# Keys written to memory by tile, contiguous marks as weights, and batches of 15 tiles (seven gathered) in 208 steps instead of 16 in 195

## The reference

```python
msg = relu(x[src] + edge_attr_32)                 # 400000 x 32
agg = segment_sum(msg, dst, num_segments=12500)   # 12500 x 32
h = (1.0 + eps[0]) * x + agg
x = layernorm(x + h @ W.T + b, axis=-1)
```

## Time and profile before

| what | value |
|---|---|
| median of three runs | 3029.05 us (3026.18 to 3032.44) |
| span of the profiled execution, first to last instruction | 2071.9 us |
| own time of the profiled execution | not recorded beside the span |
| TensorE busy | 2016.0 us, 46449 matmuls |
| VectorE, ScalarE, GpSimd busy | 1648.3, 1565.9 and 1519.9 us |
| TensorE's granted clock over the span | 0.993 of full speed |

### The profile page before, as it was taken

The page is one execution under the profiler, slowest core; times in us unless marked ns, Lnnn a source line. Parts: engine busy times, 40 slices in busy tenths (PEclk is TensorE's granted clock), DMA queues, the critical chain, the costliest instruction groups (busy, mean ns, idle before and its releaser), DMA issues. The chain is left out here.

```text
span 2071.9 us, 117127 instructions
## 1 busy us (share of the span) xinstructions
PE 2016.0 (97%) x46449; PEld 1922.5 (93%) x46449; DVE 1648.3 (80%) x4231; ACT 1565.9 (76%) x1616; POOL 1519.9 (73%) x1571
## 2 busy tenths in 40 slices
PE   4899999999999999999999999999999999999997
PEld 3899999999999999999999999999999999999994
DVE  7888778888888778888888877888888887788875
ACT  5777777777777777777777777777777777777773
POOL 6577777777777777777777777777777777777770
PEclk9999999999999999999999999999999999999998
DMA  6344454444444444544444444444444444444441
GB/s 163 84 111 113 113 114 114 112 110 109 110 111 112 112 113 114 114 110 110 110 110 110 114 112 113 112 114 109 110 110 110 111 113 113 111 114 114 110 110 34
DMA packets 236283, 228.68 MB, mean 110 GB/s; under 512 B 104218, under 2 KB 185556, under 8 KB 236062
## 3 DMA queue, kind: packets, MB, share of 16 engines
q1 hardware_dynamic: 186177, 202.59, 33.4%
q0 software_dynamic: 50080, 25.74, 13.3%
HBM read 225.43 MB, written 2.71 MB: 110 GB/s over the span
## 5 line engine op out<-in xcount | busy, mean ns | idle before, releaser
L541 POOL DMA_INDIRECT rows_all<-in_x,index x1565 | 1519.4, 971 | 502.8 <-issue 476.5
L1173 PE MATMUL found<-table,oh 128*128 128x128 bf16 x18720 | 1241.3, 225 | 11.5 <-issue 2.5
L1173 PEld LDWEIGHTS found<-table,oh 128*128 128x128 bf16 x18720 | 1168.1, 144 | 43.6 <-issue 20.0
L1012 ACT ACTIVATE oh<-keys,minus_lanes 128x1024 bf16<-128x1024 f16 x195 | 224.2, 1150 | 307.3 <-PE found L1173 294.5
L1154 PE MATMUL l<-xparts,oh 128*57 128x96 bf16 x18720 | 436.2, 207 | 0.9 <-ACT oh L1000 0.9
L1154 PEld LDWEIGHTS l<-xparts,oh 128*57 128x57 bf16 x18720 | 409.4, 108 | 14.0 <-issue 1.1
L993 ACT ACTIVATE oh<-slots,minus_lanes 128x1824 bf16<-128x1824 f16 x195 | 351.3, 1801 | 7.1 <-DMA slots<-slot_dram 7.1
L786 DVE COPY_PREDICATED rows_all<-mask,found 128x256 f32<-128x256 uint16 x780 | 343.1, 440 | 7.6 <-issue 1.4
L968 ACT CAST table<-l 128x768 bf16<-128x768 f32 x390 | 310.9, 798 | 39.7 <-PE l L1154 24.7
L1000 ACT ACTIVATE oh<-oh 128x1824 bf16<-128x1824 bf16 x195 | 335.7, 1721 | 0.0
L780 DVE TENSOR_TENSOR mask<-iota,side 128x32 f16<-128x32 f16 x195 | 37.5, 192 | 303.1 <-PE found L1173 291.0
(11 more groups left out here) (126 smaller groups left out, 906.5 us busy)
## 6 DMA issues: line engine op xcount, KB each, us to landing
slots<-slot_dram SPq DMA_DIRECT2D x195, 456.0 KB
msg<-in_edge SPq DMA_DIRECT2D x390, 128.0 KB
keys<-key_dram SPq DMA_DIRECT2D x195, 256.0 KB
rows_all<-in_x,index POOLq DMA_INDIRECT x1565
index<-in_src SPq DMA_DIRECT2D x195, 4.0 KB
key_dram<-key SPq DMA_DIRECT2D x195, 2.0 KB
slot_dram<-slot_row SPq DMA_DIRECT2D x195, 3.6 KB
oh<-in_x SPq DMA_DIRECT2D x3, 512.0 KB, 6.2
```

Source lines behind the costliest of these rows:

```text
L541: pool.indirect_dma_start(to, None, x, bass.IndirectOffsetOnAxis(indices[:, j:j + 1], 0)).then_inc(done, 16)
L1012: nc.scalar.activation(key_marks(b), by_edge(keys[:, four, :]), ACT.Square, bias=minus_lanes[:, b:b + 1]).then_inc(keys_squared, 1)
L1173: last = nc.tensor.matmul(found[:, t * FOUND:(t + 1) * FOUND], key_marks(b)[:, :, t], table[:, b, n * FOUND:(n + 1) * FOUND],  start=(b == ...
```

## The change

The keys go to memory by tile: the write of `key` now puts a partition's eight keys 128 places apart, so that the 128 keys of a tile lie together there, in `keys` and in the marks; `oh2` loses its pitch, and a tile's weights are 128 neighbouring values. `POOLED` goes from 8 to 7, a batch from 16 to 15 tiles, and since 3125 = 5 + 208 x 15 the steps go from 195 to 208. Eight tiles a batch are looked up as before. The rest follows from the odd number of tiles.

```diff
-    POOLED = 8
+    POOLED = 7
...
-    PITCH = LOOK + 2
...
+    PAIRS = (TILES + 1) // 2
-    TURNS = [(0, 3), (3, 6), (6, POOLED)]
+    TURNS = [(0, 3), (3, 5), (5, POOLED)]
...
-        oh2 = sb("oh2", [P, KEYS, P * PITCH], BF16)
+        oh2 = sb("oh2", [P, KEYS, COLS], BF16)
...
         def key_marks(b):
-            return oh2[:, b, :].rearrange("p (e t) -> p e t", t=PITCH)[:, :, 0:LOOK]
-
-        def by_edge(values):
-            return values.rearrange("p (e t) -> p e t", t=LOOK)
+            return oh2[:, b, :]
+
+        def tile_marks(b, t):
+            return oh2[:, b, t * P:(t + 1) * P]
...
-                    sp.dma_start(key_dram[four].rearrange("(p t) -> p t", t=LOOK), key[:, two, :]).then_inc(key_written, 16)
+                    with nc.allow_non_contiguous_dma(reason="keys go to memory by tile, a partition's eight far apart"):
+                        sp.dma_start(key_dram[four].rearrange("(t p) -> p t", t=LOOK), key[:, two, :]).then_inc(key_written, 16)
...
-                    nc.vector.tensor_scalar(key_marks(b), by_edge(keys[:, four, :]), lanes[:, b:b + 1], None, ALU.is_equal).then_inc(oh2_ready, 1)
+                    nc.vector.tensor_scalar(key_marks(b), keys[:, four, :], lanes[:, b:b + 1], None, ALU.is_equal).then_inc(oh2_ready, 1)
...
-                    nc.scalar.activation(key_marks(b), by_edge(keys[:, four, :]), ACT.Square, bias=minus_lanes[:, b:b + 1]).then_inc(keys_squared, 1)
+                    nc.scalar.activation(key_marks(b), keys[:, four, :], ACT.Square, bias=minus_lanes[:, b:b + 1]).then_inc(keys_squared, 1)
...
-                                found[:, t * FOUND:(t + 1) * FOUND], key_marks(b)[:, :, t],
+                                found[:, t * FOUND:(t + 1) * FOUND], tile_marks(b, t),
```

More of the change, by code:

```diff
@@ L429, in take_nodes, with nodes_of_tile @@
             eng.wait_ge(nodes_turned, k + 1)
-            copy(rel[:, 2 * k:2 * k + 2, 0:ROWS], turned_nodes(k)[:, :, 0:ROWS]).then_inc(nodes_taken[k % 2], 1)
+            n = min(2, TILES - 2 * k)
+            copy(rel[:, 2 * k:2 * k + n, 0:ROWS], turned_nodes(k)[:, 0:n, 0:ROWS]).then_inc(nodes_taken[k % 2], 1)
+        def nodes_of_tile(h, rows, j):
+            if j < POOLED:
+                return rel_rows[0:rows, h, 0:P * POOLED].rearrange("b (p t) -> b t p", t=POOLED)[:, j, :]
+            return rel_rows[0:rows, h, P * POOLED:BATCH].rearrange("b (p t) -> b t p", t=LOOK)[:, j - POOLED, :]
         def one(ap3, b):
@@ L677, in take_all_nodes @@
             def take_all_nodes():
-                for k in range(0, TILES // 2, 2):
+                for k in range(0, PAIRS, 2):
                     take_nodes(nc.vector.tensor_copy, dve, k)
@@ L1021, in step @@
                 if not st.inside and st.s == 0:
-                    for k in range(1, TILES // 2, 2):
+                    for k in range(1, PAIRS, 2):
                         take_nodes(nc.scalar.copy, act, k)
@@ L1108, in turn_nodes @@
                 pe.wait_ge(late_taken, 1)
-                for k in range(TILES // 2):
+                for k in range(PAIRS):
                     if k >= 2:
                         pe.wait_ge(nodes_taken[k % 2], k // 2)
-                    for t in range(2):
-                        j = 2 * k + t
-                        at = j if j < POOLED else j - POOLED
+                    for j in range(2 * k, min(2 * k + 2, TILES)):
                         for h, b0, b1 in HALF_ROWS:
-                            span = rel_rows[0:b1 - b0, h, :].rearrange("b (g p t) -> b g t p", g=SPANS, t=LOOK)[:, j // POOLED, at, :]
-                            last = nc.tensor.matmul(turned_nodes(k)[:, t, b0:b1], span, ident_half[0:b1 - b0, 0:b1 - b0], start=True, stop=True)
+                            last = nc.tensor.matmul(turned_nodes(k)[:, j % 2, b0:b1], nodes_of_tile(h, b1 - b0, j), ident_half[0:b1 - b0, 0:b1 - b0], start=True, stop=True)
                     last.then_inc(nodes_turned, 1)
@@ L1125, in turn_nodes @@
                 for h in range(2):
-                    pe.wait_ge(nodes_taken[h], (TILES // 2 + 1 - h) // 2)
+                    pe.wait_ge(nodes_taken[h], (PAIRS + 1 - h) // 2)
             def prepare_weights():
```

## The result

The changed kernel takes 4670.88 us (4599.94 to 4700.07, four runs) beside 3027.61 us for the kernel before: a ratio of 1.529, 95% interval [1.5233, 1.5347]. The ratio takes only the two of the four runs that lie within 1.5% of the fastest (4599.94 and 4657.03 us) beside before; the ratio of the two medians is 1.543. It is slower by 1643 us, ten times the 168 us that I forecast.

What follows compares the result with a forecast made beforehand. TensorE was taken as the bound, in timed runs at 64.0 ns per matmul: 2665 more matmuls add 170.6 us to 3029.05, giving 3199.6, stated as 3197 us with a small second-stage gain; 8-in-10 range 3030 to 3215 us.

Steps and rivals of the forecast that it cites:

- The key write: Key write on SyncE's queue, 1024 two-byte pieces a step: between nothing and 2.5 us of delay, taken as nothing.
- My rival for it: Key write holds the slots' loop at 10.1 us a step or more: 3160 us, chance 0.07 including no weight saving.
- the loop of the slots: From L993 through the slot row's write to the load of `slots`, needed 10.09 us after L993 starts.
- The gap of 957 us: Timed median exceeds the profiled span by 957.15 us; read as a pace per matmul in timed runs, not time around the span.
- a pace of 64 ns per matmul: TensorE in timed runs: each matmul takes 64.0 ns, so 2665 more add 170.6 us and shorter weight loads save nothing.
- the likeliest case: Pace per matmul on TensorE in timed runs: 3197 us, own range 3160 to 3215, chance 0.58.
- The sum in the profile's terms: Whole kernel: +131 us for thirteen more steps, -110 us for contiguous weights, +21 us in all; span 2093 us.
- The loop through the picks: Last `found` matmul, mask and picks on VectorE, then second stage set the step; saved segment sums are worth nothing.
- Gathers and marks hidden: GpSimd's seven gathers, 8.9 us against a 9.6 us step, hide behind TensorE; marks on VectorE and ScalarE cost nothing.
- The sign: Whole kernel: slower with chance 0.83 less 0.01 for tails, within 0.2% 0.04, faster 0.14.

Runs made afterwards that it cites:

- the write mended: Changed kernel, keys turned by a small matmul and written in 256-byte pieces: 2935.01 us, ratio 0.9503; or with the key write by edge: 2940.36 us, 0.9531; both slow pace.
- the by-edge write: Changed kernel with its key write put back to 128 pieces of 16 bytes, output wrong: 2105.11 us, ratio 1.014, beside a before of 2076.14 us.

## Why the prediction was wrong, step by step

**The key write.** This is the step that failed: "I take nothing for it, because pieces of two bytes move far less than those of 512", with an upper bound of 2.5 us a step. The bound came from a load whose pieces go each to a place of its own. It priced how long the pieces keep the DMA engines from other work, and that part was small indeed: 8 ns a piece in the changed kernel's packet records. What the runs showed in its place is the landing: 15.6 us in the changed kernel by the measure above, against 1.4 us for by-edge pieces, and a harm of 10.8 us a step even with nobody waiting for the write. My rival for it saw only the loop of the slots, 3160 us, with a chance of 0.07; I never asked what else shares the way to memory with the write.

**The gap of 957 us.** Wrong as used. The 957 us are inside the execution, as I guessed, but in stops of TensorE at fixed places of its loop, not as a pace of 64 ns per matmul; that instructions are what it lacks there is still a guess. By that pace 2665 more matmuls were to cost 170.6 us; with the write mended the 15-tile kernel took 5% less than before, not 5.6% more. So the likeliest case would have missed even without the write. The Trainium skill's 62 ns for each MATMUL with hardware decoding off (TensorE: Matmul & The Clock Gate, section "Wait — 56ns, not 53.3ns?") are no floor in any trace here: the slow one did 71 matmuls in 1.73 us, 24 ns each.

**The sum in the profile's terms.** Right but for the write, and for the quick pace alone: I said a span of 2093 us, a step of 9.6 and a run of 24 in 1.50 us; with the by-edge write it was 2101.9 us, 9.62 and 1.50 us. The terms: saving 0.47 us a step where I took 0.53, from 55.7 to 56.0 ns where I took 55. That strided weights cost nothing, as I read the Trainium skill's "packed or strided" (same page, section "Weight-path perf modes — Fast Weight Load (FWL) and DoubleRow"), the measurement denies: about 60 ns against 56, the mean weight load 144 against 98 ns.

**The loop through the picks.** Right: the second stage still starts 0.23 us after the last pick, with one segment sum less.

**Gathers and marks hidden.** Right in the mended kernel. In the changed one GpSimd waited for TensorE most of all, 1394.2 us in the second stage alone.

**The sign** was right by luck: at the pace of the first comparison the same kernel with a mended write is faster than before, and only the write that I priced at nothing made it slower.

## What to carry to other kernels

Ask of a scattered write not only how many pieces it has but how many of them fall within the same few hundred bytes: 256 such pieces of two bytes a step cost this kernel 1744 us, 1024 spread ones at most 12.5 us (single runs). Turn the data on the chip first, where one small matmul does it. And where the time and a profile of the same kernel differ by half, get a profile at that pace before reasoning on either.

## What the runs showed of the hardware that I had not expected

A transfer that nobody waits for doubled a kernel's time (2076.14 to 4186.82 us), with stops of TensorE of up to 9.7 us, though each of its pieces kept a DMA engine only 9 ns on the average. "Issue" in the middle of a run of one line's matmuls is the row to look for. And one and the same program ran at 2076 or at 3025 to 3090 us, steady to 0.3% within each series.
